# In the last layer of a four-layer graph network, the gather's last third also waits for steps of the sums

## The chip, the cores and the metric

The kernel runs on one core of a Trainium2 chip. What is measured is the device time of one execution in microseconds (us), and all times of the profile come from one profiled execution of the same program. A core has five engines with instruction streams of their own: TensorE (PE in the profile, its weight loads PEld), VectorE (DVE), ScalarE (ACT), GpSimd (POOL) and SyncE (SP), and sixteen DMA engines which they all feed. The engines meet at semaphores only.

## The reference

Four graph layers on 6250 nodes of 128 features, 206250 edges sorted by target. The change lies in the last layer, an attention that keeps the 8 strongest edges of each node for each of 4 heads:

```python
h = (x @ W).reshape(N, H, C)                    # 4 heads of 32
x_j = h[col]                                    # one row for every edge
e = leaky_relu(score_i[row] + score_j[col], 0.2)
e = where(is_among_the_8_largest_of(row), e, -inf)
ez = exp(e - segment_max(e, row)[row])
alpha = ez / segment_sum(ez, row)[row]
out = elu(segment_sum(alpha * x_j, row))
x = layernorm(x + out)
```

## The kernel before, in words

Edges are handled in 1664 tiles of 128, four tiles to a group, so there are `GS` = 416 groups. `stage_last_layer` holds the whole last layer after the node table. Its work on the engines, in order of time:

- **Gather** (POOL, L1612, the tile `z_xg`): for each tile one indirect DMA fetches 128 rows of 136 floats from `v.table` in HBM. The 1664 issues stand in a plain, unrolled loop. Four buffers (`U = 4`) hold one group each. At the start of a group POOL waits for the store that frees the buffer (`s_st`), and for `s_look`: group `g` waits for `g * 5 // 2` of the looks, at most all 416.
- **Store** (SP, L1624): as soon as a group's four tiles are there, 256 KB go to `gathered` in HBM.
- **Looks** (PE L1644 and L1645, DVE L1759 and L1764): 416 steps that find each edge's score by products with one-hot tiles. They count `s_look`.
- **Top 8** (mainly DVE, L721 to L809): nine passes of segmented scans over all edges' scores. PE turns small tiles for them. After them 52 transposes on PE (L1662), each copied by ACT (L1705), bring the weights into the order of the edges.
- **Sums** (`prepare`, `add` and `sums`): 464 steps (`KS`; 416 groups, and 48 of them visited once more where a block of 128 nodes ends). For step `k`, ACT loads a group's rows from `gathered` into `z_buf` (L1715) and copies the weights beside them (L1718). DVE makes the one-hot tile (`z_oh`, L1832) and the weighted rows (`z_wrow`, L1836). PE forms four products in float32, each in two passes, so that a step has 8 weight loads and 8 matmuls (L1672), and counts `s_mm`. DVE adds the result (`acc`, L1848).

What ties the sums together: DVE's order is prepare(k), then add(k-3). add(k-3) waits for `s_mm` to reach k-2. PE may start the products of step `k` once add(k-4) is done (four PSUM halves). ACT waits for `s_mm` only eight steps back, and does not load step `k` before the store of group `k` has landed.

After the sums `stage_update` normalizes, and the result is written.

Of the kernel before, what the change touches and what calls it, by code (L numbers as in the profile page):

```python
# [40 lines left out]
GS = TS // G  # L41
# [1506 lines left out]
def stage_last_layer(nc, v, gathered, steps, acc):  # L1548
# [13 lines left out]
    s_z, s_oh, s_w, s_wc, s_mm, s_add = (sem("z_" + n) for n in ("zero", "oh", "w", "wc", "mm", "add"))  # L1562
# [6 lines left out]
    with ExitStack() as mem:  # L1569
# [23 lines left out]
        with nc.Block() as block:  # L1593
            @block.gpsimd
            def _(pool):
                for b in range(NB):
                    nc.gpsimd.indirect_dma_start(
                        out=v.firsts[:, :], out_offset=bass.IndirectOffsetOnAxis(ap=v.base[:, b:b + 1], axis=0),
                        in_=v.scores[:, b, H:2 * H], in_offset=None).then_inc(s_first, 16)
                pool.wait_ge(s_fl, 48)  # L1600
                nc.gpsimd.indirect_dma_start(
                    out=start[:, :], out_offset=None, in_=v.table[:, :],
                    in_offset=bass.IndirectOffsetOnAxis(ap=cur[:, 0:1], axis=0)).then_inc(s_start, 16)
                for t in range(TS):
                    g, j = t // G, t % G
                    u, use = g % U, g // U
                    if j == 0 and g:

                        pool.wait_ge(s_look, min(g * 5 // 2, GS))
                    if j == 0 and use:  # L1610
                        pool.wait_ge(s_st[u], use * 16)
                    nc.gpsimd.indirect_dma_start(  # L1612
                        out=xg[:, u, j, :], out_offset=None, in_=v.table[:, :],
                        in_offset=bass.IndirectOffsetOnAxis(ap=v.dsti[:, t:t + 1], axis=0)).then_inc(s_xg[u], 16)
# [553 lines left out]
```

## Time and profile before

| | us |
|---|---|
| median of 3 runs | 12312.5 (12300.32 to 12318.69) |
| time of the profiled execution | 12319.95 |
| its span in the profile | 12318.2 |
| looks, with the gather beside them | to 9979 |
| top 8 and the transposes, with the gather beside them | 9979 to 10712 |
| sums, the gather still running | 10712 to 11549 |
| sums alone | 11575 to 12235 |
| update and output | 12235 to 12318 |

The stages' borders are read from the first and last instructions of their lines. Busy time of an engine is the time in its compute or gather instructions. PEclk is the granted TensorE clock as a share of 2.4 GHz: 0.50 is 1.2 GHz. Ends of matmuls are modelled in the profile, their starts are not.

### The profile page before, as it was taken

What the parts mean: (1) busy time and instruction counts of PE and PEld (TensorE: products, weight loads), DVE (VectorE), ACT (ScalarE), POOL (GpSimd) and SP (SyncE); (2) the same over time, 40 slices, a digit from 0 to 9 for tenths busy, and PEclk for the clock granted to TensorE, in tenths of its full rate; (3) what the DMA queues carried; (4) which work ended last, traced back from release to release, by engine and by line L of the source; (5) the groups of instructions that cost most, each with busy time, mean ns of one, the idle gap of its engine ahead of it and who ended that gap; (6) DMA issues with size and microseconds to landing.
All of it is one profiled execution on the core that took longest, in us unless ns stands there. A gap on an engine that the chain in (4) does not pass through costs nothing. (4 is left out here: it accounts for less than half of the span.)

```text
span 12318.2 us, 202597 instructions
## 1 busy us (share of the span) xinstructions
PE 6923.2 (56%) x43540; PEld 5743.1 (47%) x43541; DVE 6711.3 (54%) x13147; ACT 1613.7 (13%) x4982; POOL 6398.0 (52%) x7772
## 2 busy tenths in 40 slices
PE   4777777776583555555555526996467730100375
PEld 3666666665473444444444424773256630000364
DVE  5333333334677555555555525887455689600499
ACT  1000000000211322222222200111100000000011
POOL 2555555551384344444444455882166678877300
PEclk9999999999797777777777758997588865555698
DMA  3555555553373344444444459993077742344454
GB/s 98 161 159 157 161 160 159 161 159 114 106 207 92 113 129 131 129 128 132 129 130 127 139 155 179 269 268 85 28 179 192 192 123 73 92 113 108 127 168 127
DMA packets 2114487, 1742.89 MB, mean 141 GB/s; under 512 B 377268, under 2 KB 1838645, under 8 KB 2114213
## 3 DMA queue, kind: packets, MB, share of 16 engines
q1 hardware_dynamic: 1220182, 819.70, 22.8%
q10 hardware_dynamic: 708032, 472.39, 15.8%
q0 software_dynamic: 186160, 449.72, 13.0%
q14 instruction: 94, 0.76, 0.0%
q8 instruction: 19, 0.31, 0.0%
HBM read 1289.54 MB, written 453.29 MB: 141 GB/s over the span
## 5 line engine op out<-in xcount | busy, mean ns | idle before, releaser
L1152 POOL DMA_INDIRECT sorted<-m_rows,srci x1612 | 1574.4, 977 | 1768.6 <-ACT srci L1256 978.0
L1612 POOL DMA_INDIRECT z_xg<-table,srci x1664 | 1888.1, 1135 | 725.5 <-issue 473.3
L452 POOL DMA_INDIRECT g_xg<-table,srci x1612 | 1581.1, 981 | 1105.8 <-DVE g_es L554 628.3
L1201 PE MATMUL m_psl<-m_part,m_ohtb 128*128 128x100 bf16 x4836 | 472.1, 251 | 1175.7 <-DVE m_mul L1340 725.7
L471 PE MATMUL g_psg<-g_wg,g_eT 128*128 128x136 f32 x3224 | 1047.0, 472 | 135.3 <-issue 134.3
L1672 PE MATMUL z_ps<-z_wrow,z_oh 128*128 128x132 f32 x3712 | 575.0, 302 | 957.8 <-issue 472.2
L488 PE MATMUL g_psx<-scores,g_hot 128*128 x3608 | 840.3, 362 | 446.1 <-DVE e_score L579 267.7
L488 PEld LDWEIGHTS g_psx<-scores,g_hot 128*128 128x128 f32 x3608 | 806.5, 328 | 477.8 <-issue 476.5
L1484 PE MATMUL n_ps<-n_row,n_oh 128*128 128x257 f32 x3712 | 880.3, 389 | 192.6 <-DVE n_row L1460 170.4
L1201 PEld LDWEIGHTS m_psl<-m_part,m_ohtb 128*128 128x128 bf16 x4836 | 408.5, 123 | 1227.3 <-issue 978.0
L1672 PEld LDWEIGHTS z_ps<-z_wrow,z_oh 128*128 128x128 f32 x3712 | 488.6, 203 | 1044.3 <-issue 972.9
L471 PEld LDWEIGHTS g_psg<-g_wg,g_eT 128*128 128x128 f32 x3224 | 776.2, 322 | 331.7 <-issue 331.6
L1644 PE MATMUL z_ps<-z_tab,z_ohlo 128*128 128x200 bf16 x4992 | 720.7, 279 | 352.8 <-DVE z_e L1764 267.2
L1484 PEld LDWEIGHTS n_ps<-n_row,n_oh 128*128 128x128 f32 x3712 | 678.8, 190 | 394.1 <-issue 310.9
L1211 PE MATMUL m_psx<-held,m_hot 128*128 x3608 | 689.3, 347 | 214.5 <-DVE m_rows L1365 129.7
L1333 DVE TENSOR_TENSOR m_part<-m_rest,m_part 128x200 bf16<-128x200 f32 x403 | 147.8, 367 | 1180.4 <-ACT m_part L1252 738.2
L823 POOL TENSOR_TENSOR ag_wrow<-ag_buf,e_score 128x512 f32<-128x512 f32 x451 | 467.2, 1057 | 474.3 <-DMA ag_buf<-gated 374.2
L1211 PEld LDWEIGHTS m_psx<-held,m_hot 128*128 128x128 f32 x3608 | 597.2, 249 | 248.6 <-issue 243.4
L1644 PEld LDWEIGHTS z_ps<-z_tab,z_ohlo 128*128 128x128 bf16 x4992 | 503.6, 110 | 422.6 <-issue 330.5
L1764 DVE TENSOR_REDUCE z_e<-z_ps 128x800 f32 (+1 forms) x416 | 411.0, 988 | 465.6 <-DMA ag_buf<-gated 305.3
L569 DVE TENSOR_SCALAR g_hot<-g_keys,node 128x512 f32<-128x512 int32 x451 | 232.1, 515 | 655.1 <-DMA g_keys<-dst_row 286.9
L511 ACT ACTIVATE g_gate<-g_psg 128x512 f32<-128x512 f32 x403 | 240.6, 597 | 2457.9 <-remote 1497.3
(412 smaller groups left out, 13950.8 us busy)
## 6 DMA issues: line engine op xcount, KB each, us to landing
n_row<-sorted SPq DMA_DIRECT2D x464, 520.0 KB, 4.7
z_buf<-gathered ACTq DMA_DIRECT2D x464, 256.0 KB
g_keys<-dst_row ACTq DMA_DIRECT2D x451, 256.0 KB
ag_buf<-gated SPq DMA_DIRECT2D x451, 256.0 KB, 3.2
m_keys<-dst_row ACTq DMA_DIRECT2D x451, 256.0 KB
gathered<-z_xg SPq DMA_DIRECT2D x416, 256.0 KB
gated<-g_y SPq DMA_DIRECT2D x403, 256.0 KB
g_eT<-in_attr_t SPq DMA_DIRECT2D x402, 256.0 KB
```

The costliest lines, as they stand in the source:

```text
L452: nc.gpsimd.indirect_dma_start(out=xg[:, u, j, :], out_offset=None, in_=v.table[:, :], in_offset=bass.IndirectOffsetOnAxis(ap=v.srci[:, t: ...
L471: last = nc.tensor.matmul(psg[u % 2][:, h, j * W:(j + 1) * W], eT[:, u, (h * H + j) * P:(h * H + j + 1) * P], wg[:, :], start=False, stop= ...
L488: last = nc.tensor.matmul(psx[u % 2][:, j * X8:(j + 1) * X8], hot_t[:, u, j * P:(j + 1) * P], flat(v.scores[:, ds(b, 1), :]), start=True, ...
L823: engine.tensor_tensor(wrow[:, u, :, 0:C].rearrange("p t (h c) -> p t h c", h=heads), buf[:, u, :, :].rearrange("p t (h c) -> p t h c", h= ...
L1152: nc.gpsimd.indirect_dma_start(out=v.sorted[:, :], out_offset=bass.IndirectOffsetOnAxis(ap=place[:, t:t + 1], axis=0), in_=rows[:, u, j, : ...
L1201: nc.tensor.matmul(to, ohtb[:, u, j * P:(j + 1) * P], before, start=(n == 0), stop=False)
L1211: last = nc.tensor.matmul(psx[u % 2][:, j // 2, (j % 2) * WH:(j % 2 + 1) * WH], hot_t[:, u, j * P:(j + 1) * P], flat(held[:, ds(b, 1), :]) ...
L1484: last = nc.tensor.matmul(ps[u % 4][:, 0:ROW], oh[:, u, j, :], row[:, u, j, 0:ROW], start=(j == 0), stop=(j == G - 1))
L1612: nc.gpsimd.indirect_dma_start(out=xg[:, u, j, :], out_offset=None, in_=v.table[:, :], in_offset=bass.IndirectOffsetOnAxis(ap=v.dsti[:, t: ...
L1644: nc.tensor.matmul(to, ohlo[:, u, edges], tab[:, n, :, :], start=(n == 0), stop=False)
L1672: last = nc.tensor.matmul(bank[u % 4 // 2][:, u % 2, 0:width], oh[:, u, j, :], wrow[:, u, j, 0:width], start=(j == 0), stop=(j == G - 1))
L1764: nc.vector.tensor_reduce(e[:, ds(g * G, G), :].rearrange("p (b t) h -> p b (t h)", b=2), bank[u % 2][:, :, 0:2 * H * NBX].rearrange("p b ...
```

## The change

A third wait at the start of a group. The number `done` is zero or less up to g = 270 and adds nothing there. From g = 271 it is 3, 6, 9, 12, 16 and so on, 3.2 for each group, up to 380 at g = 389. From g = 390 on it is `g - 8`, that is 382 to 407. So 145 of the 416 groups get the wait. No instruction moves on any engine, and all 1664 gathers, 416 stores and 464 steps stay.

```diff
                     if j == 0 and g:
 
                         pool.wait_ge(s_look, min(g * 5 // 2, GS))
+
+
+                    done = min((g - GS + 146) * 16 // 5, g - 8)
+                    if j == 0 and done > 0:
+                        pool.wait_ge(s_mm, done)
                     if j == 0 and use:
                         pool.wait_ge(s_st[u], use * 16)
                     nc.gpsimd.indirect_dma_start(
```

## Rows read from the trace of the kernel before

**Rows 1.** Busy time of every engine in four stretches, with instruction counts, clock, DMA.

```profile
core 0: us, PE busy (x) PEld busy (x) DVE busy (x) ACT busy (x) POOL busy (x), PEclk, DMA share, GB/s
...
9000.00:9950.00 950.00, 668.53 (x6078) 599.56 (x6076) 570.32 (x1140) 0.00 (x0) 583.92 (x608) 0.87 0.76 191
10100.00:10600.00 500.00, 7.68 (x25) 3.18 (x25) 494.79 (x444) 0.00 (x0) 417.68 (x271) 0.50 0.29 73
10800.00:11500.00 700.00, 65.42 (x248) 56.43 (x248) 51.72 (x95) 6.90 (x32) 532.04 (x506) 0.50 0.44 109
11600.00:12200.00 600.00, 441.86 (x3073) 373.50 (x3073) 574.29 (x1153) 82.83 (x384) 0.00 (x0) 1.00 0.58 168
```

**Rows 2.** The gather (L1612) before and after the sums begin: stretch, busy (count), clock, DMA.

```profile
8900.00:10712.00 1812.00, 1252.89 (x1055) 0.71 0.55 140
10712.00:11549.00 837.00, 635.18 (x610) 0.50 0.45 113
```

**Rows 3.** Two sums' steps while the gather runs: start, duration, engine, line, idle before.

```profile
11004.27 0.21 ACT L1718 ACTIVATE z_wrow<-z_e 128x16 f32 x1 [22.27 <-DMA sorted<-t_loops]
11004.29 0.29 DVE L1848 TENSOR_TENSOR acc<-acc,z_ps 128x132 f32 x1 [20.46 <-DMA sorted<-t_loops]
...
11005.94 0.68 DVE L1836 TENSOR_TENSOR z_wrow<-z_buf,z_e 128x512 f32<-128x512 f32 x1
...
11006.82 2.12 PE L1672 MATMUL z_ps<-z_wrow,z_oh 128*128 128x132 f32 x8 [20.79 <-issue]
...
11026.72 0.22 ACT L1718 ACTIVATE z_wrow<-z_e 128x16 f32 x1 [22.24 <-DMA sorted<-t_loops]
11026.83 0.29 DVE L1848 TENSOR_TENSOR acc<-acc,z_ps 128x132 f32 x1 [20.20 <-DMA sorted<-t_loops]
```

**Rows 4.** DVE's prepare (L1836), its add (L1848), PE's matmuls (L1672), counted to 11540.

```profile
10712.00:11540.00 828.00, 27.28 (x40) 0.50 0.45 113
```

```profile
10712.00:11540.00 828.00, 10.52 (x36) 0.50 0.45 113
```

```profile
10712.00:11540.00 828.00, 83.97 (x320) 72.75 (x320) 0.50 0.45 113
```

**Rows 5.** ACT's copies of single PE transposes, just before the sums, timeline.

```profile
10704.24 0.43 ACT L1705 ACTIVATE z_e<-z_ps 128x128 f32<-128x128 f32 x1 [2.36 <-remote]
...
10707.04 0.43 ACT L1705 ACTIVATE z_e<-z_ps 128x128 f32<-128x128 f32 x1 [2.37 <-remote]
...
10709.84 0.43 ACT L1705 ACTIVATE z_e<-z_ps 128x128 f32<-128x128 f32 x1 [2.37 <-remote]
```

**Rows 6.** Around one group of the gather among the looks, timeline.

```profile
9398.98 0.97 POOL L1612 DMA_INDIRECT z_xg<-table,srci  x1 [0.30 <-issue]
...
9401.41 0.25 PE L1645 MATMUL z_ps<-z_mask,z_ohhi 128*128 128x200 bf16 x1
9401.50 0.94 POOL L1612 DMA_INDIRECT z_xg<-table,srci  x1 [0.30 <-issue]
9403.70 0.99 DVE L1764 TENSOR_REDUCE z_e<-z_ps 128x800 f32 x1 [3.12 <-DMA ag_buf<-gated]
9403.98 0.94 POOL L1612 DMA_INDIRECT z_xg<-table,srci  x1 [1.53 <-DMA ag_buf<-gated]
```

**Rows 7.** The gather among the looks (9000 to 9950): count, busy, mean ns, idle before.

```profile
L1612 POOL DMA_INDIRECT z_xg<-table,srci x608 | 584.3, 961 | 366.2 <-issue 142.3 <-DMA ag_buf<-gated 123.4 <-PE z_ps L1645 100.5
```

**Rows 8.** Gathers beside DVE's weighted rows, in the sums' first steps, timeline.

```profile
10718.45 0.69 DVE L1836 TENSOR_TENSOR z_wrow<-z_buf,z_e 128x512 f32<-128x512 f32 x1 [1.22 <-DMA z_buf<-gathered]
10718.86 1.10 POOL L1612 DMA_INDIRECT z_xg<-table,srci  x1 [0.30 <-issue]
...
10720.16 0.68 DVE L1836 TENSOR_TENSOR z_wrow<-z_buf,z_e 128x512 f32<-128x512 f32 x1
10720.26 1.40 POOL L1612 DMA_INDIRECT z_xg<-table,srci  x1 [0.30 <-issue]
...
10724.46 0.94 POOL L1612 DMA_INDIRECT z_xg<-table,srci  x1 [0.30 <-issue]
```

**Rows 9.** The end of the gather and what follows it, timeline.

```profile
11547.81 1.24 POOL L1612 DMA_INDIRECT z_xg<-table,srci  x1 [0.87 <-issue]
11564.57 0.22 ACT L1718 ACTIVATE z_wrow<-z_e 128x16 f32 x1 [20.81 <-DMA sorted<-t_loops]
...
11574.49 0.29 DVE L1848 TENSOR_TENSOR acc<-acc,z_ps 128x132 f32 x1 [7.61 <-DMA sorted<-t_loops]
```

**Rows 10.** All adds of the sums (L1848): first and last start.

```profile
L1848 DVE TENSOR_TENSOR acc<-acc,z_ps x464: 279/283/293, 10736.0 to 12235.5; 128x132 f32 x155
```

## The prediction, made before the changed kernel ran

> **What bounds the kernel now.** I read the busy times by stretch first [rows 1]. Among the looks every engine works. In the top 8 DVE is busy for 99% of the time, so it bounds. The stretch 10800 to 11500 is odd: PE is busy for 9%, DVE 7%, the DMA engines 44%, and only the gather on POOL looks busy (76%). It holds 32 sums' steps (ACT's 32 copies) in 700 us, 21.9 us for each. The fourth stretch, without a gather, holds 384 in 600 us, 1.56 us for each, with DVE at 96%. So the sums bound the end in both, and beside the gather they run fourteen times slower.
>
> Next, one slow step [rows 3]. DVE's add waits 20 us and ACT's copy 22 us, and both go on at the same moment. Both wait for `s_mm`, PE's count. DVE's prepare and PE's products follow within 2.5 us, and then nothing happens. The counts show that it isn't the products of this step that are awaited: by 11540 PE has issued 320 matmuls, that is 40 steps, and DVE has prepared 40, but only 36 are added [rows 4]. PE is four steps ahead of what the others see, which is all that the PSUM halves allow. So PE's signals arrive late, one step's for about 22.4 us. The releaser printed beside these waits (a DMA of another stage) can't be meant.
>
> How late? The transposes just before the sums are copied every 2.80 us [rows 5], and each is one weight load and one matmul. A sums' step is 8 of each: 8 x 2.80 = 22.4 us. And 506 gathers in 700 us are one every 1.38 us [rows 1], half of 2.80. While gathers follow each other unbroken, about one PE instruction's completion gets through for each gather. With a pause it is different. Among the looks POOL stops at each group's start. The gather that starts at 9401.50 ends at 9402.44; DVE's reduce, which waits for products issued at 9401.41 and before, starts at 9403.70, 1.26 us after the gather's end, and POOL goes on at 9403.98 [rows 6]. DVE's 1140 instructions there are three for each look [rows 1]: 380 looks, 2.5 us each, get through beside 608 gathers in 950 us. After the very last gather the backlog needs longer: adds flow freely only at 11574.5, 25 us after it [rows 9].
>
> **What the change does here.** At 10712 POOL has issued 1055 gathers and stands in group 263 [rows 2]. Groups to 270 have no new wait, so the top 8 is untouched. From g = 271 POOL has to stop until the sums have gone on 3.2 steps for each group. The wait bites: before, 610 gathers (152 groups) passed while 42 steps were made. Each stop is a pause in which PE's signals can arrive. Behind the waiting instruction stand only POOL's own gathers; the stores on SP and, for steps near the group's number, ACT's loads depend on them.
>
> The length P of one period (a group and its 3.2 steps) decides everything. It is made of these terms:
> - Four gathers, issued one after the other. Among the looks one takes 0.961 us [rows 7] and 0.30 us follows it [rows 6]: 4 x 1.26 = 5.05 us.
> - The pause in which the signals arrive. The 608 gathers are 152 groups, 6.25 us each, so 1.20 us are left for it. I take the same.
> - Gathers held up by DVE. One that starts while DVE multiplies `z_wrow` ends late: 1.10 us where the product had 0.28 us to go, 1.40 where it had 0.58; the one that starts clear of it takes 0.94 [rows 8]. DVE spends 3.2 x 0.68 = 2.2 us of a period in that instruction, a third of it; a third of the four gathers waits some 0.2 us: 0.3 us.
> - Steps that are not ready when the pause comes. DVE and PE can work four steps ahead during a burst, and need 3.2. DVE's part is 3.2 x 1.56 = 5.0 us, less than the period. But PE takes 2.12 us for a step at 1.2 GHz [rows 3], 3.2 x 2.12 = 6.8 us, and 1.15 us at 2.4 GHz (442 us for 384 steps, rows 1). Among the looks the clock was granted at 0.87 with PE 70% busy, so I expect mostly the high level, and 0.05 us for this.
>
> Sum: P = 5.05 + 1.20 + 0.3 + 0.05 = 6.6 us. Bounds: 6.25 as among the looks [rows 1] (a little less if the pauses merge, 6.1), and 8.6 if the gathers are slowed as in the top 8, where 271 in 500 us are 1.845 us apart: 4 x 1.845 + 1.2. The looks are nearer, since DVE is not full in the new stretch either.
>
> The time, from the profile's own clock:
> - 10712 to g = 271: 1084 - 1055 = 29 gathers at 1.38 us = 40 us, so 10752.
> - Groups 271 to 389: 119 x 6.6 = 785 us, so 11537. 380 steps are allowed by then.
> - Groups 390 to 415 wait for only one step more each. Four steps may pass in one pause, so a group needs 4 x 1.38 + 1.2/4 = 5.8 us: 26 x 5.8 = 151 us, so 11688.
> - About 408 steps are done. 56 are left, alone: 56 x 1.56 = 87 us, and 5 us for the backlog (before: 25 after 150 unbroken groups [rows 9]), so 11780.
> - From the last add (12235.5 [rows 10]) to the end of the span are 82.7 us, and the profiled execution took 1.75 us more than its span: 11780 + 84 = 11864.
>
> The profiled execution of before (12319.95) stands 7.5 us above the median of its runs, less than the run-to-run spread of 18 us, so I leave it there: 11864.
>
> **A rule of the Trainium skill against a row.** Gathers that start during a DVE multiply end late [rows 8], and in the top 8 they are 1.845 us apart [rows 1]. The Trainium skill (SBUF — State Buffer, "Who interferes with whom") says that a tensor_tensor with both inputs in SBUF contends only with GpSimd instructions that read SBUF and not with the writing of descriptors; by it the 0.3 us would fall away. Here the trace doesn't agree: 1.40 us against 0.94.
>
> **Rivals.**
> 1. As forecast, P between 6.1 and 7.1: 145 periods times 0.5 us either way, 11790 to 11935. For it: the looks are the same pattern (a group of gathers, a pause, PE's signals), with only two PSUM banks of depth where the sums have four. The case without any hold-up by DVE lies in it: P = 6.25 gives 11864 - 119 x 0.35 = 11822. Chance 0.68.
> 2. DVE's work holds the gathers up as in the top 8: P = 8.6, and 7.4 + 0.3 in the last 26 groups: 10752 + 1023 + 200 + 92 + 84 = 12151. For it: DVE will be two thirds busy with instructions of the same kind. Against: a gather waits only when it starts in one of 0.68 us, and those of the top 8 last 1.0 to 1.9 us. Something between the two (11935 to 12100) is possible too, through the slow TensorE clock above all: 0.15 for between, 0.06 for the full case.
> 3. Slower. The burst and the steps shut each other out: nothing of the sums runs ahead during a burst, and each period is 5.05 + 1.2 + 3.2 x 1.56 = 11.2 us. Then 10752 + 119 x 11.2 + 26 x 7.8 + 92 + 84 = 12464. It decides from P = 9.8 on, where 145 periods use up what is saved. For it: each stop of POOL is real idle time and 145 groups get one. Against: 40 steps prepared to 36 added [rows 4] shows that the work ahead is done during bursts. Chance 0.06.
> 4. The wait is met already when it is reached, and nothing changes: it would need 3.2 steps per group, where before there were 42 to 152. Chance 0.02. What is left, 0.03, is faster than 11790: the signals pass sooner and P is under 6.1.
>
> **How the numbers follow.** The forecast is the first case's centre, 11864. The range takes that case with both ends and the part between 1 and 2, so 11790 to 12100, 0.83. Faster by over 0.2% (about what a measurement of this kernel can tell from no change, 25 us): cases 1, 2, between and the fast rest, 0.92. Within it 0.02. Slower 0.06.
>
> **What would show it.** In the profile of after: the sums begin near 10712 as before; the stretch 10800 to 11500 holds some 330 steps instead of 32, and POOL about 106 groups, with DVE at 65 to 75% and a granted clock over 0.8; POOL's idle time before a group is 1.2 to 1.6 us, put down to the sums; the last gather starts near 11690; adds alone afterwards for about 90 us at 1.56 us. If gathers there take 1.4 us and more on average, rival 2 is it. If POOL's idle time before a group is 5 us, rival 3. I am wrong at the root if the adds still wait 20 us in short stretches: then the pauses don't free PE's signals.

## The result, and the profile after

The changed kernel takes 11821.12 us (median of 4 runs, 11818.57 to 11826.61), the kernel before 12309.51 (4 runs, 12300.32 to 12318.69): a ratio of 0.9606, with the 95% interval from 0.9593 to 0.9618. The profiled execution took 11818.62 us, its span is 11816.9. The forecast was 11864, in a range from 11790 to 12100.

All lines below the edit stand five higher in the changed kernel: the gather is L1617, the sums' products L1677, the weighted rows L1841, the add L1853. First the same stretches as in [rows 1], busy time of every engine with instruction counts, then clock, DMA share and GB/s:

```profile
9000.00:9950.00 950.00, 673.51 (x6092) 603.91 (x6093) 571.96 (x1141) 0.00 (x0) 586.03 (x609) 0.86 0.77 192
10100.00:10600.00 500.00, 8.17 (x27) 3.55 (x27) 494.82 (x455) 0.00 (x0) 417.74 (x271) 0.50 0.29 73
10800.00:11500.00 700.00, 466.76 (x2786) 415.86 (x2784) 534.13 (x1046) 74.55 (x346) 461.95 (x436) 0.84 0.77 213
```

The looks and the top 8 are as they were. In the third stretch PE's 248 matmuls have become 2786 and ACT's copies 346 instead of 32, the clock went from 0.50 to 0.84, and POOL made 436 gathers instead of 506. So 14% fewer gathers in that time bought eleven times as many steps.

The costliest groups of that stretch (line, engine, operation, count, busy, mean ns, then the idle time before them and what ended it):

```profile
L1677 PE MATMUL z_ps<-z_wrow,z_oh 128*128 128x132 f32 x2786 | 467.0, 327 | 233.1 <-issue 105.5 <-DVE z_oh L1837 58.1 <-DVE acc L1853 36.2
L1617 POOL DMA_INDIRECT z_xg<-table,srci x436 | 463.2, 1062 | 238.4 <-issue 237.4 <-PE z_ps L1677 0.9
...
L1853 DVE TENSOR_TENSOR acc<-acc,z_ps 128x132 f32 x349 | 99.8, 286 | 60.4 <-PE z_ps L1677 33.5 <-DMA sorted<-t_loops 14.7 <-issue 11.2
```

In [rows 3] one add had waited 20 us. Here 349 adds wait 60 us together. The gather's idle time is put down to "issue" nearly always, although the new wait is on PE's count: the name of a releaser is of little use on POOL here.

Now the end of the last layer by the forecast's own borders, first with the gathers (L1617) counted, then with the adds (L1853):

```profile
10690.00:10737.00 47.00, 26.88 (x29) 0.54 0.52 141
10737.00:11500.00 763.00, 503.48 (x476) 0.83 0.77 214
11500.00:11646.00 146.00, 99.13 (x102) 0.58 0.53 140
```

```profile
10690.00:10737.00 47.00, 1.44 (x5) 0.54 0.52 141
10737.00:11500.00 763.00, 108.37 (x379) 0.83 0.77 214
11500.00:11646.00 146.00, 7.45 (x26) 0.58 0.53 140
11646.00:11735.00 89.00, 15.46 (x54) 0.91 0.56 152
```

476 gathers are 119 groups, in 763 us: one period is 6.41 us. (The first border, 10737, lies behind the four gathers of g = 271, so these are the groups 272 to 390.) The timeline of POOL shows what the first stop, before g = 271, costs (start, duration, and in brackets the idle time before):

```profile
10719.49 0.95 POOL L1617 DMA_INDIRECT z_xg<-table,srci  x1 [0.30 <-issue]
10732.32 0.95 POOL L1617 DMA_INDIRECT z_xg<-table,srci  x1 [11.89 <-issue]
```

The last gather before it ends at 10720.4. The adds, from the same place in DVE's timeline:

```profile
10713.24 0.29 DVE L1853 TENSOR_TENSOR acc<-acc,z_ps 128x132 f32 x1 [9.88 <-issue]
10731.58 0.29 DVE L1853 TENSOR_TENSOR acc<-acc,z_ps 128x132 f32 x1 [16.33 <-DMA sorted<-t_loops]
10733.52 0.28 DVE L1853 TENSOR_TENSOR acc<-acc,z_ps 128x132 f32 x1
10734.98 0.28 DVE L1853 TENSOR_TENSOR acc<-acc,z_ps 128x132 f32 x1
```

PE's signals need 11 us of rest on POOL to arrive, and then the adds follow each other in 1.5 us. That is some nine times the pause of 1.20 us that the forecast counted on; but such a long stop comes once. From g = 272 to 389 POOL rests 1.1 to 2.9 us before 69 of the 118 groups, and before the other 49 not at all (only the 0.30 us that stand between any two gathers). So most rows of gathers between two rests are eight long, not four. Two rests in a row, each before a group:

```profile
11100.13 0.95 POOL L1617 DMA_INDIRECT z_xg<-table,srci  x1 [2.52 <-issue]
...
11106.70 0.95 POOL L1617 DMA_INDIRECT z_xg<-table,srci  x1 [1.82 <-issue]
...
11107.87 0.29 DVE L1853 TENSOR_TENSOR acc<-acc,z_ps 128x132 f32 x1
...
11109.33 0.29 DVE L1853 TENSOR_TENSOR acc<-acc,z_ps 128x132 f32 x1
...
11110.99 0.29 DVE L1853 TENSOR_TENSOR acc<-acc,z_ps 128x132 f32 x1
...
11113.39 0.94 POOL L1617 DMA_INDIRECT z_xg<-table,srci  x1 [1.70 <-issue]
```

Between two rests the adds go on at 1.5 us beside the gathers, too. So it isn't that signals pass only while POOL rests. But in rows of eight the lateness begins to show again: of the 376 distances between adds from 10740 to 11500, 56 are over 2.5 us, and most of these end 7 to 12 us after the last rest. In the last 26 groups, which ask for one step more each, POOL stops only five times, once for 6.5 us, and there too 26 adds pass in 146 us.

### The profile page after: what moved, and what is told of

Same layout as the page of the kernel before. It is cut to its first block and busy times, and to the rows that moved or that the text cites. A ratio compares the mean times of both kernels' runs of the same rounds, so it can differ in the third digit from the quotient of the medians.

```text
span 11816.9 us, 202597 instructions
## 1 busy us (share of the span) xinstructions
PE 6985.8 (59%) x43540; PEld 5822.2 (49%) x43541; DVE 6725.7 (57%) x13147; ACT 1612.9 (14%) x4982; POOL 6409.5 (54%) x7772
## 5 line engine op out<-in xcount | busy, mean ns | idle before, releaser
L1617 POOL DMA_INDIRECT z_xg<-table,srci x1664 | 1887.6, 1134 | 847.7 <-issue 599.5
L1677 PE MATMUL z_ps<-z_wrow,z_oh 128*128 128x132 f32 x3712 | 630.3, 329 | 424.0 <-issue 173.5
L1677 PEld LDWEIGHTS z_ps<-z_wrow,z_oh 128*128 128x128 f32 x3712 | 560.3, 231 | 494.1 <-issue 352.4
```

What stands on the lines that cost most here:

```text
L1617: nc.gpsimd.indirect_dma_start(out=xg[:, u, j, :], out_offset=None, in_=v.table[:, :], in_offset=bass.IndirectOffsetOnAxis(ap=v.dsti[:, t: ...
L1677: last = nc.tensor.matmul(bank[u % 4 // 2][:, u % 2, 0:width], oh[:, u, j, :], wrow[:, u, j, 0:width], start=(j == 0), stop=(j == G - 1))
```

## The experiments

**One thing has to be known first.** The kernel before was run beside each batch of experiments, and it took either 12297 to 12312 us, or 9684 to 9700 us, with nothing between. On one and the same chip it took 9699.66, 9684.26 and 12296.96 at three times. So every kernel is compared only with the run of the kernel before from its own batch, and each batch says something about one of two regimes. In the text they are "12300" and "9700". Each experiment is a single run of its kernel.

### In the 9700 regime

Four kernels were meant to take the change apart. The first is the kernel before with half of the products left out (PE has 8 instructions per step instead of 16; the sums lack these products):

```diff
-                    for j in range(G):
+                    for j in range(0, G, 2):
...
-                              ... start=(j == 0), stop=(j == G - 1))
+                              ... start=(j == 0), stop=(j == G - 2))
```

> The kernel before (no wait on the sums), but the sums form only two of a step's four products (the other two are left out), so a step has 4 weight loads and 4 matmuls instead of 8 and 8. DVE's work, the loads and the gather stay. Theory A (while gathers follow each other unbroken, PE's completions get through one for each gather): a step beside the gather takes 8 x 1.40 = 11.2 us instead of 22.4, some 75 steps are done when the gather ends instead of 42, and the whole is 33 x 1.56 = 50 us faster than before, near 12265. Rival B (the slow step is a matter of the loads or stores beside the gather's DMAs, or of the semaphore alone, one for each step): 22.4 us a step stay, 42 steps, and the time of before within 10 us.

Measured: 9690.69 beside 9699.66. The second puts a fixed filling of a scratch tile in the place of the counted wait, at the start of the last 146 groups:

```diff
+                    if j == 0 and g >= GS - 146:
+                        if g > GS - 146:
+                            pool.wait_ge(s_idle, g - GS + 146)
+                        nc.gpsimd.memset(idle[:, :], 0.0).then_inc(s_idle, 1)
```

> The kernel before, no wait on the sums; from g = 270 on POOL fills a scratch tile of 1040 floats (some 0.95 us) at each group's start, so the gather is broken up without being paced by the sums. Theory A (a break in the gather is what lets PE's signals pass): a period of 5.05 + 0.3 + 1.25 = 6.6 us, in which up to four steps pass; the sums catch up with the stores before the gather ends near 11700, and the whole takes some 11880. Rival B (only POOL really idle, or the pace of the sums, helps): steps stay near 22 us and the 145 fills are added in vain, 12318 - 6 + 145 x 1.25 = 12490, less the 10 more steps that pass meanwhile, 12475.

Measured: 9842.70 beside 9699.66. The third and the fourth keep a part of the change:

```diff
-                    if j == 0 and done > 0:
+                    if j == 0 and g % 4 == 3 and done > 0:
```

> The changed kernel with the new wait at every fourth group only (g = 271, 275, ...), with the same number there. The same pace is asked, in bursts of 16 gathers. Theory A with the depth of four PSUM halves: in a burst of 16 gathers (22 us) no more than five steps pass, the other 8 of 12.8 need 8 x 1.56 = 12.5 us of idle POOL, so 34 us for four groups, 8.6 a group instead of 6.4: 119 x 2.2 = 260 us more than the changed kernel, near 12080. If the backlog after a long burst takes 25 us as at the gather's end, up to 12 a group and slower than before. Rival B (the breaks are only a cost, and what helps is that steps and gathers are interleaved at that pace): fewer breaks, 5.8 a group, 11750.

Measured: 9684.47 beside 9699.66.

```diff
-                    if j == 0 and done > 0:
+                    if j == 0 and g < 390 and done > 0:
```

> The changed kernel without the wait of the last 26 groups (g = 390 to 415). Theory A: these 26 groups run unbroken, 144 us as now, but only some 6 steps pass in them instead of 26, and after the gather the backlog needs up to 25 us. So 20 steps x 1.56 = 31 us and some 20 us of backlog more than the changed kernel: 11870. Rival B (the last groups' waits cost more than they bring): equal or faster, 11820 or under.

Measured: 9692.94 beside 9699.66.

None of these says anything about the theories, since the thing that they dispute isn't there. Three groups of the third kernel, each with its first and last start, show it (gather, weighted rows, add):

```profile
L1617 POOL DMA_INDIRECT z_xg<-table,srci x1664: 940/947/7816, 7116.5 to 9511.0; - x185
```

```profile
L1841 DVE TENSOR_TENSOR z_wrow<-z_buf,z_e x464: 676/684/745, 8468.0 to 9597.8; 128x512 f32<-128x512 f32 x155
...
  DMA z_buf<-gathered: 325.4, 112
```

```profile
L1853 DVE TENSOR_TENSOR acc<-acc,z_ps x464: 277/286/296, 8473.9 to 9600.1; 128x132 f32 x155
```

The weighted rows wait 325 us for rows that the gather has yet to deliver, and the adds wait for no signal of PE at all (8 us of idle time before all 464 of them). The sums stay on the gather's heels until it ends at 9511, and 90 us later they are through. There the gather is the bound, and 780 of them fit into 1030 us:

```profile
8480.00:9510.00 1030.00, 577.78 (x3251) 495.48 (x3249) 630.14 (x1218) 86.52 (x401) 792.44 (x780) 0.73 0.76 205
```

The waits of the change are then met when POOL reaches them (its idle time before a gather is 0.3 us at most there), which is why its parts give nothing. The fixed filling does cost, and to the letter: 146 times 0.98 us is 143 us, the measured difference.

```profile
L1615 POOL MEMSET z_idle<- x146: 978/983/990, 8770.9 to 9664.3; 128x1040 f32 x146
```

### The change once more, and the repeats

To see whether the measured gain comes back, the changed kernel was run unchanged.

> The changed kernel itself, beside the kernel before. The runs e1 to e4 came from a chip on which the kernel before takes 9699.66 us, not 12312, and there the gather and the sums did not disturb each other: DVE waited for loads only. On such a chip Theory A (the change pays by letting PE's late signals pass) expects nothing from the change, since no signal is late: within 20 us of before. Rival B (the pace of gathers and sums is worth something in itself, through transfers or the order of loads) expects a gain there too, some 4% in ratio. On a chip where the kernel before takes 12310, both expect 11820.

Measured: 11832.89 beside 12312.08, a ratio of 0.9611. Three of the first four kernels were repeated on another chip.

> The same kernel as e1 (before, with two of a step's four products left out, so 4 weight loads and 4 matmuls a step), meant for a chip where the kernel before takes 12310. Theory A: a step beside the gather takes 8 x 1.40 = 11.2 us instead of 22.4, some 75 steps are done when the gather ends instead of 42, 12318 - 50 = near 12265. Rival B (late for each step, by the semaphore or by the loads): 22.4 us a step and the time of before within 10 us. If the kernel before takes 9700 again: as e1, 9690.

> The same kernel as e2 (before, plus a fill of some 0.98 us on POOL at each group's start from g = 270 on, no wait on the sums). Where the kernel before takes 12310, Theory A: a period of 5.05 + 0.3 + 1.3 = 6.65 us in which signals pass, the sums catch up with the stores, 11880. Rival B (only an idle POOL lets the signals pass, not one that is busy with something else): steps stay near 22 us, 12475. If the kernel before takes 9700: as e2, 9843.

> The same kernel as e3 (changed, with the new wait at every fourth group only). Where the kernel before takes 12310, Theory A with four PSUM halves of depth: 34 us for four groups against 25.7 in the changed kernel, near 12080; with the backlog of 25 us after each burst, up to 49 us for four groups, and then slower than before. Rival B (interleaving alone): 11750. If the kernel before takes 9700: as e3, 9684.

Measured: 9696.06, 9843.19 and 9698.13 beside 9700.15, the 9700 regime again. And two more times:

> Once more the kernel of e1 and f1 (before, with two of a step's four products left out: 4 weight loads and 4 matmuls a step), which both met a chip where the kernel before takes 9700 and no signal is late. Where it takes 12310, Theory A (one PE completion gets through for each gather): 11.2 us a step beside the gather, some 75 steps when it ends, near 12265. Rival B (late for each step, by the semaphore or the loads): 22.4 us a step, within 10 us of before. Where it takes 9700: 9690 as twice before.

Measured: 9692.24 beside 9684.26.

> Once more the kernel of e2 and f2 (before, plus a fill of 0.98 us on POOL at the start of each group from g = 270 on, and no wait on the sums), hoping for a chip where the kernel before takes 12310. There, Theory A (any break in the gather lets PE's signals pass): a period of 6.65 us, the sums catch up with the stores, near 11880. Rival B (a POOL that is busy with something else is no break; it has to be idle): steps stay near 22 us, 12475. Where the kernel before takes 9700: 9843 as twice before.

Measured: 9834.92 beside 9690.59. In 9700 half the products are within 0.1% of all, and the fixed filling costs 143 to 144 us each time. These five repeats show no more than that.

### In the 12300 regime

The last two kernels therefore hold several experiments each, one behind the other along the groups, so that one run in the 12300 regime answers all of them. The first is the kernel before with half the products left out in every second step (8 and 16 instructions of PE alternate) and four kinds of fixed filling:

```diff
+                    size = 0
+                    if 312 <= g < 336:
+                        size = 1040
+                    elif 336 <= g < 356:
+                        size = 256
+                    elif 356 <= g < 380:
+                        size = 0 if g % 2 else 1040
+                    elif 380 <= g:
+                        size = 0 if g % 4 else 1040
+                    if j == 0 and size:
+                        ...
+                        nc.gpsimd.memset(idle[:, 0:size], 0.0).then_inc(s_idle, 1)
```

> The kernel before, without the wait on the sums, with several experiments in one run. Odd steps of each eight form two of their four products (the other two are left out): 4 weight loads and 4 matmuls instead of 8 and 8. POOL fills scratch at some groups' starts: g = 312 to 335 each group 0.98 us; 336 to 355 each group 256 floats, some 0.3 us; 356 to 379 every second group 0.98 us; from 380 every fourth group 0.98 us. Where the kernel before takes 12310, Theory A expects: to g = 311 adds that come alternately 22.4 and 11.2 us apart; then periods of 6.6 us with up to four steps each (so about 90 steps in 24 groups); with the short fill fewer or none, between the two; with every second group four steps for two groups in 12.5 us; with every fourth four steps for four groups in 23.4 us; in all near 12090. Rival B (late for each step and not for each PE instruction): 22.4 us for odd and even steps alike to g = 311. Rival C (only an idle POOL lets signals pass): steps stay at 11 to 22 us to the end of the gather, near 12330. Where the kernel before takes 9700, both: nothing waits for signals, and the fills cost what they last where the gather bounds, 24 x 0.98 + 20 x 0.3 + 12 x 0.98 + 9 x 0.98 = 50 us, near 9750.

Measured: 12267.39 beside 12296.96. First the alternating steps, with gathers unbroken (the adds, L1866 there):

```profile
10752.39 0.29 DVE L1866 TENSOR_TENSOR acc<-acc,z_ps 128x132 f32 x1 [20.39 <-remote]
10763.59 0.29 DVE L1866 TENSOR_TENSOR acc<-acc,z_ps 128x132 f32 x1 [8.79 <-issue]
10786.07 0.29 DVE L1866 TENSOR_TENSOR acc<-acc,z_ps 128x132 f32 x1 [20.47 <-issue]
10797.31 0.29 DVE L1866 TENSOR_TENSOR acc<-acc,z_ps 128x132 f32 x1 [9.20 <-issue]
```

11.2 us and 22.5 us in turn: 1.40 us for each instruction of PE, 8 or 16 of them. What is late is counted in PE's instructions, not in steps. This is shown, and it was the reading of [rows 5].

Rival B is out with this. Then the fillings, with steps of 12 instructions on average. The adds of the same kernel in four stretches: without filling; the first 18 or so groups with 0.98 us of it; the last ones of these; and all behind (0.3 us in each group, then 0.98 us in every second and in every fourth):

```profile
10730.00:10945.00 215.00, 3.80 (x13) 0.50 0.49 124
10945.00:11070.00 125.00, 2.34 (x8) 0.50 0.38 95
11070.00:11105.00 35.00, 2.31 (x8) 0.50 0.56 144
11105.00:11545.00 440.00, 8.19 (x28) 0.50 0.46 115
```

With a fill of 0.98 us in each group the adds stay at one in 16 us for 125 us, and only then, within a few groups, they come at one in 4.4 us:

```profile
11074.92 0.29 DVE L1866 TENSOR_TENSOR acc<-acc,z_ps 128x132 f32 x1 [8.38 <-remote]
...
11088.54 0.29 DVE L1866 TENSOR_TENSOR acc<-acc,z_ps 128x132 f32 x1 [6.36 <-remote]
11090.78 0.28 DVE L1866 TENSOR_TENSOR acc<-acc,z_ps 128x132 f32 x1
11095.15 0.29 DVE L1866 TENSOR_TENSOR acc<-acc,z_ps 128x132 f32 x1 [2.29 <-PE z_ps L1690]
```

With 0.3 us, and with 0.98 us in every second or fourth group, 28 adds in 440 us are 15.7 us for each, nearly as slow as the 16.5 without any (apart from three gaps of 7 to 9 us after 11209). So the forecast's theory of a pause (a rest of about 1.2 us in each group lets the signals pass) falls in this form: it had given 12090 for this kernel, 177 us too little. Rival C (only an idle POOL helps) is out as well, since the quick adds come beside fills with no idle time before them.

The break was even longer than the fill. In the slow 125 us most fills start late, up to 2.6 us and 1.0 us on average, so that with the fill and 0.15 us behind it 2.1 us lie between the gathers of two groups; in the change it is 1.2 us on average. One of them:

```profile
10993.45 0.96 POOL L1625 MEMSET z_idle<- 128x1040 f32 x1 [2.59 <-remote]
```

What a fill waits for, with the looks long done, is POOL's own count of the fill before, which ended 7.5 us earlier. In the 9700 regime none of the 146 fills had idle time before it. So in this kernel not only PE's signals are late, but POOL goes on late as well; whether it is the same cause no run shows.

What fits these stretches is a backlog: unbroken issue of gathers builds something up, breaks take it down bit by bit, and as long as it stands PE's signals come at 1.40 us each. That something behind POOL needs longer for a gather than POOL for issuing one is a guess.

The last kernel tests the backlog with the complete products. It is the changed kernel, with its wait in three forms: as it is up to group 330, at every fourth group up to 387, and not at all from 388 on.

```diff
-                    if j == 0 and done > 0:
+                    if j == 0 and done > 0 and (g < 331 or (g < 388 and g % 4 == 3)):
```

> The changed kernel, with all products, but its wait for the sums stands in three forms: groups 271 to 330 as in the change, groups 331 to 387 only at every fourth group (with the same number), and none from 388 on. Where the kernel before takes 12300: Both theories expect some 6.4 us per group in the first part (as measured in the changed kernel) and in the last part about 5.5 us per group with one step in 22 us, and so some 79 steps alone after the gather. They differ in the middle part, where 16 gathers follow each other unbroken and then the sums have 12.8 steps to catch up. Theory 1, as I see it now (what stands behind POOL takes 1.38 us for a gather and POOL issues one in 1.26, so a backlog of 16 x 0.12 = 2 us builds up in a burst, and PE's signals are late only by that): the steps go on during the burst, four groups take 22 to 26 us, 5.6 to 6.5 us per group, and the whole takes 11850 to 11900. Theory 2 (in any unbroken burst one PE completion passes per gather, from its first gather on, so the burst brings one step and the four that are ahead, and the other 8 follow at 1.56 us): four groups take 22 + 1 + 8 x 1.56 = 35 us or more, 8.9 us per group, and the whole takes 12030 to 12080. Where the kernel before takes 9700 both expect 9680 to 9700.

Measured: 11984.53 beside 12306.0, between the two expectations (11850 to 11900, and 12030 to 12080). The stretches of the three forms, and the time after the gather (every engine, as above):

```profile
10750.00:11136.00 386.00, 261.71 (x1536) 234.53 (x1536) 295.30 (x579) 42.07 (x195) 251.43 (x241) 0.83 0.78 216
11136.00:11621.00 485.00, 245.50 (x1445) 219.55 (x1446) 275.44 (x541) 39.05 (x181) 226.07 (x228) 0.72 0.59 162
```

```profile
11621.00:11761.00 140.00, 18.55 (x77) 15.84 (x75) 14.67 (x26) 1.51 (x7) 105.90 (x112) 0.51 0.47 121
```

The first form gives 386/60 = 6.43 us per group, as in the changed kernel. The second needs 485 us for 57 groups, 8.5 us each or 34 us for four, which theory 2 had put at 35; theory 1 (22 to 26) is out. The third gives 140/28 = 5.0 us per group, where both had expected 5.5: its gathers stand 1.25 us apart, and the adds 22.5 us. One run thus shows the adds quick with the wait and slow again without it. And the pace of 1.40 us per signal isn't that of the gathers: it was the same with gathers 1.25 us apart here, 1.30 (165 in 215 us) in the kernel with the fillings and 1.38 in the kernel before. The transposes of [rows 5], 2.80 us apart, also lie beside gathers 1.25 us apart (10 in the 12 us from 10700), not 1.38.

That the row is unbroken doesn't make the signals late by itself. In the top 8 of the kernel before the gathers are 1.845 us apart [rows 1], without a rest too, and DVE reads a product of PE 0.07 us after its end:

```profile
10135.96 1.54 POOL L1612 DMA_INDIRECT z_xg<-table,srci  x1 [0.30 <-issue]
10137.45 0.23 PE L762 MATMUL z_ps<-ident,zs_cf 4*128 4x4 f32 x1
...
10137.75 0.13 DVE L746 COPY zs_in<-z_ps 128x4 f32<-128x4 f32 x1
```

There PE also has few instructions (25 matmuls in 500 us), and no run separates this from the wider spacing.

Theory 2 isn't quite right either in what happens within a burst: over the thirteen bursts of 16 gathers 5 to 8 adds pass in one, where it had five. The adds of one period of four groups (16 gathers from 11172.5 to 11193.6, then 11.7 us of rest):

```profile
11179.97 0.29 DVE L1853 TENSOR_TENSOR acc<-acc,z_ps 128x132 f32 x1
...
11182.97 0.29 DVE L1853 TENSOR_TENSOR acc<-acc,z_ps 128x132 f32 x1 [1.45 <-PE z_ps L1677]
...
11187.41 0.29 DVE L1853 TENSOR_TENSOR acc<-acc,z_ps 128x132 f32 x1 [2.29 <-DMA sorted<-t_loops]
...
11196.12 0.29 DVE L1853 TENSOR_TENSOR acc<-acc,z_ps 128x132 f32 x1 [6.20 <-DMA sorted<-t_loops]
```

The first gathers disturb nothing (an add every 1.5 to 1.8 us), then the gaps grow to 3.0, 4.4 and 8.7 us, and the next add comes 2.5 us after the burst. In the thirteen bursts the quick adds end 4 to 7.5 us after the first gather, that is after three to six gathers, the last gap is 6.5 to 14.2 us, and the next add comes 1.1 to 3.1 us after the burst's end. After longer rows it takes more. 68 gathers stand between one of 7.5 us, with which the top 8 ends, and the first stop of the change: the next add comes 11.1 us after them, 10.5 in the repeated run and 11.0 in this kernel. After the last 29 groups here (116 gathers) it is 13 us (11761 to 11774.5). In the kernel before, after 649 gathers since that of 7.5 us, it is 15.6 us (11549.05 to 11564.67), and 25 until the adds flow freely [rows 9]. So the delay that a row leaves grows with its length at first, but far less than in proportion, and behind long rows a part of each figure is chance, since an add is due there only every 11 or 22 us: in the kernel with the fillings the next add came 1.4 us after the gather's end. From 16 gathers to 68 the growth is clear, and it fits a backlog; beyond, it isn't. What the queue is that fills, if it is one, and why PE's signals stand in it, no run here shows.

## Why the prediction was right, point by point

- **What bounds.** That beside the gather the sums wait for PE's signals, not for PE, was right: with the same products, the adds' idle time in 10800 to 11500 went from nearly all of it to 60 us. That it is 1.40 us for each instruction of PE is shown by the alternating steps. That it is "one for each gather" was wrong: 1.38 and 1.40 lay together by chance, the pace stays when the gathers' pace is another, and beside the very transposes of [rows 5] it was another. It did no harm to the sum, which didn't use it.
- **The period.** Forecast 6.6 us, measured 6.41 in 119 groups. Four gathers with what holds them up: 4 x (1.062 + 0.30) = 5.45 us, forecast 5.05 + 0.3 = 5.35. The rest at the group's start: 238.4/109 = 2.19 us of idle time per group, less 4 x 0.30, is 0.99 us, forecast 1.20 + 0.05. So the gathers' hold-up beside DVE was sized well, and the pause was put 0.25 us too long. But 0.99 us is a mean over groups with rests up to 2.9 us and groups without any. The forecast had one pause behind each group; that the mean comes near it is in part luck. The steps by themselves (3.2 x 1.5 = 4.8 us) are shorter than the period, as said.
- **The hold-up by DVE** shows in the last kernel as well. Beside running steps gathers take 1.15 to 1.35 us; later in the same burst, when DVE has run dry, 0.94:

```profile
11174.99 1.32 POOL L1617 DMA_INDIRECT z_xg<-table,srci  x1 [0.30 <-issue]
11176.61 1.34 POOL L1617 DMA_INDIRECT z_xg<-table,srci  x1 [0.30 <-issue]
...
11182.64 0.94 POOL L1617 DMA_INDIRECT z_xg<-table,srci  x1 [0.30 <-issue]
```

  The trace again shows the hold-up. It does not show that the rule of the Trainium skill cited in the prediction (SBUF — State Buffer, "Who interferes with whom") fails: that rule lets such a multiply contend with GpSimd instructions that read SBUF, and each gather takes its 128 row numbers from the tile `v.dsti` in SBUF. Whether this reading or the writing of descriptors is held up no run here separates.
- **The mechanism behind the pause** was the weak step. "Each stop is a pause in which PE's signals can arrive" took the rests of the looks for enough by their length. With the fixed fill the breaks were 2.1 us on average, more than the change's, and the adds stayed slow for some 18 groups. What differs in the change is that its stop is a counted one: at the first stop POOL waits until the steps are really there, 11.9 us long, and the later ones keep the lateness small. Which of the two does it is not shown: a fixed fill after one long first stop wasn't tried. The forecast's time line had no such first stop. It cost 12 us, and was made good by chance: 24 gathers at 1.25 us lay before it (30 us), where the forecast had 29 at 1.38 (40 us).
- **The time line.** The sums begin 22 us earlier, at 10690 against 10712 (the first weighted rows at 10693.6 against 10715.8), which has nothing to do with the change, since no wait of it is reached before. In the repeated run they begin at 10716.2, and it took 11832.89. Then 42 us to the first gather of g = 271 (forecast 40), 765 for the 119 groups to g = 389 (785), 149 to the gather's end (151), 89 (92) and 84. The differences, -22 + 2 - 20 - 2 - 3, are -45: 11864 becomes 11819, and 11818.62 was measured. Half of the miss is the earlier start, which moves from run to run, and half the period.
- **Rival 2** (P = 8.6) would have shown gathers of 1.4 us and more; they take 1.062. **Rival 3** (11.2) would have shown rests of 5 us; they are 1 us on average. But its mechanism is real: with the wait at every fourth group only, the burst outgrows what can run ahead, POOL rests 11 to 17 us, and the period is 8.5 us per group. What decides between the two is the number of gathers between two stops: mostly 8 or 4 in the change (43 and 21 of the 71 rows from 10740 to 11500), 16 there. **Rival 4** (the wait is met already) is out in the 12300 regime, and is just what the kernels with parts of the change show in the 9700 regime, where they moved nothing. Whether the full change gains or costs there wasn't tried.
- **What would show it.** Nearly all came: 349 steps (forecast 330), 109 groups (106), DVE at 76% (65 to 75), a clock of 0.84 (over 0.8), 1.23 us of idle time before a group on average (1.2 to 1.6, though 49 of 118 groups had none), 89 us of adds alone. The last gather started at 11644.8 (11690), by the differences above. The releaser of POOL's rests was "issue", not the sums.

## What to carry to other kernels

When an engine has done its work and others see it tens of microseconds later, beside an unbroken row of indirect gathers, the gathers are worth breaking: not by a rest of fixed length, but by a wait on the progress of the work that starves, often enough that what piles up between two stops stays small (four to eight gathers here; sixteen cost a third more per group). Where the disturbance wasn't there, the runs with a part of the waits cost nothing, since the sums kept up with the number asked for, and a fixed fill cost its full length. And run the old kernel beside the new one each time: here it had two durations, the longer 27% above the shorter.

## What the runs showed of the hardware that was not expected

- In the longer of the kernel's two durations, completions of PE's instructions reach the other engines at 1.40 us each while gathers follow each other unbroken, at mean spacings of 1.25 to 1.38 us; with a counted stop every few gathers, a step of 16 of them passes in 2.0 us. In the top 8, with gathers 1.845 us apart and little work on PE, they weren't late.
- The first three to six gathers of a row after a long rest slow no add. From its end to the next add it is 1.1 to 3.1 us after 16 gathers, 10.5 to 11.1 after 68, 13 after 116 and 15.6 after 649 (25 until the adds flow freely).
- POOL's own short fills start up to 2.6 us late there, too.
- The kernel before took 9684 to 9700 us or 12297 to 12319 us, and on one chip both 9684 and 12297. In the shorter one no signal of PE was seen late beside the gathers, in the last layer's looks either: they took 696 us there and 1085 us in the changed kernel in the longer one. The layers before are longer as well: the looks begin at 7070 us in the one and at 8865 in the other. Both lines are those of their first products, the shorter first:

```profile
L1649 PE MATMUL z_ps<-z_tab,z_ohlo x4992: 246/249/374, 7069.9 to 7765.7; 128*128 128x200 bf16 x200
```

```profile
L1649 PE MATMUL z_ps<-z_tab,z_ohlo x4992: 246/249/374, 8864.8 to 9950.2; 128*128 128x200 bf16 x200
```

  What sets the regime is open. These matmuls' own durations are nearly the same in both (246/249/374 ns); the time between them differs.
